# A mixture of experts in a fused kernel: GpSimd's scatter six tiles behind its gather in place of eight

## What is computed

```python
logits = t @ Wg.T + bg                              # t: 4096 tokens x 256, after a layer norm
topw, topi = jax.lax.top_k(jax.nn.softmax(logits), 2)   # 2 of 8 experts
topw = topw / jnp.sum(topw, axis=-1, keepdims=True)
...
h = t @ w1e.T                                       # 256 -> 512
gate, up = jnp.split(h, 2, axis=-1)
o = (jax.nn.silu(gate) * up) @ w2e.T                # 256 -> 256
acc = acc + ce[:, None] * o                         # ce: the token's weight for this expert
```

## Time and profile before

| | us |
|---|---|
| median of 3 runs | 1506.12 (1502.98 to 1509.09) |
| the profiled execution | 1513.09 |
| its span | 1511.3 |
| PE busy | 1179.3 (78% of the span) |
| DVE busy | 902.4 (60%) |
| ACT busy | 619.1 (41%) |
| GpSimd busy | 550.5 (36%) |

### The profile page before, as it was taken

One profiled execution on the slowest core, in us unless ns is written; L12 is line 12 of the kernel. 1 busy time (PEld: TensorE's weight loads), 2 busy tenths in 40 slices (PEclk: granted clock), 3 DMA queues, 4 the chain that ended last, 5 costly groups with the idle time before them and its releaser, 6 DMA issues. The chain is left out here.

```text
span 1511.3 us, 35117 instructions
## 1 busy us (share of the span) xinstructions
PE 1179.3 (78%) x13860; PEld 807.7 (53%) x13861; DVE 902.4 (60%) x1889; ACT 619.1 (41%) x1319; POOL 550.5 (36%) x536
## 2 busy tenths in 40 slices
PE   5999999953888888367988989797987539888860
PEld 3566666642666766134544545454545427676750
DVE  4677776757444544456668585766853474444445
ACT  2333333213344444143636446363652324444436
POOL 1333333120566665224051341405311216666640
PEclk9999999967899999588999989999997869999995
DMA  7122222039322222100000000000000482222238
GB/s 291 42 87 85 85 85 71 29 115 376 107 87 87 83 84 76 56 28 3 29 3 29 30 2 30 3 29 3 2 2 3 154 314 83 85 89 83 84 93 303
DMA packets 62424, 125.88 MB, mean 83 GB/s; under 512 B 7632, under 2 KB 43216, under 8 KB 59344
## 3 DMA queue, kind: packets, MB, share of 16 engines
q1 hardware_dynamic: 48464, 86.20, 16.2%
q0 software_dynamic: 13824, 37.77, 7.9%
HBM read 79.90 MB, written 44.04 MB: 82 GB/s over the span
## 5 line engine op out<-in xcount | busy, mean ns | idle before, releaser
L996 POOL DMA_INDIRECT ffn_xs<-xn_rows,ffn_from_row x144 | 140.0, 972 | 168.2 <-DVE ffn_to_row L1371 79.7
L1002 POOL DMA_INDIRECT y_rows<-ffn_ys,ffn_to_row x144 | 142.5, 990 | 84.7 <-DVE ffn_ys L1410 59.9
L1153 PE MATMUL ffn_ps_h<-ffn_w_high,ffn_xst 128*128 x576 | 161.3, 403 | 1.2 <-DVE ffn_xst L1404 0.6
L1394 DVE TENSOR_TENSOR ffn_act_in<-ffn_silu_g,ffn_ps_h 128x256 f32<-128x256 f32 x144 | 60.4, 420 | 160.1 <-ACT ffn_silu_g L1036 99.7
L1036 ACT ACTIVATE ffn_silu_g<-ffn_ps_h 128x256 f32<-128x256 f32 x144 | 56.4, 392 | 164.7 <-PE ffn_ps_h L1153 134.0
L1172 PE MATMUL ffn_ps_o<-ffn_w,ffn_act_t 128*128 x288 | 120.5, 441 | 0.5 <-DVE ffn_act_t L1399 0.5
L1153 PEld LDWEIGHTS ffn_ps_h<-ffn_w_high,ffn_xst 128*128 128x128 f32 x576 | 100.8, 194 | 21.5 <-issue 2.6
L1162 PE MATMUL ffn_ps_a<-ffn_constants,ffn_act_in 128*128 128x128 f32 x288 | 56.6, 278 | 55.2 <-DVE ffn_act_t L1399 55.2
L1735 POOL TENSOR_TENSOR rec_mixed_w<-rec_mixed_w,rec_xnt 128x512 f32<-128x512 f32 x16 | 17.2, 1091 | 219.3 <-DVE rec_mixed_w L2510 219.3
L2030 PE MATMUL rec_odd<-rec_mixed_w,home 128*128 128x512 f32 (+1 forms) x96 | 59.7, 760 | 45.2 <-DVE rec_mixed_r L2510 40.8
L1153 PE MATMUL ffn_ps_h<-ffn_w_low,ffn_xst 128*128 x288 | 91.2, 398 | 0.0
(11 more groups left out here) (320 smaller groups left out, 2824.2 us busy)
## 6 DMA issues: line engine op xcount, KB each, us to landing
home<-y_rows SPq DMA_DIRECT2D x20, 512.0 KB, 5.4
ffn_w_high<-w_split SPq DMA_DIRECT2D x8, 1024.0 KB, 8.4
ffn_w_low<-w_split SPq DMA_DIRECT2D x8, 1024.0 KB, 10.9
ffn_w<-w_split SPq DMA_DIRECT2D x8, 1024.0 KB, 13.9
ret_w_raw<-in_f_w SPq DMA_DIRECT2D x12, 512.0 KB, 6.4
w_split<-ret_w_high SPq DMA_DIRECT2D x12, 512.0 KB, 2.7
w_split<-ret_w_low SPq DMA_DIRECT2D x12, 512.0 KB, 4.4
xn_rows<-home SPq DMA_DIRECT2D x10, 512.0 KB, 12.3
```

The lines of the kernel that those rows point to most:

```text
L996: pool.indirect_dma_start(xs[:, n % UNROLL, :], None, xn_rows[:], bass.IndirectOffsetOnAxis(ap=from_row[:, n:n + 1], axis=0)) \
L1002: pool.indirect_dma_start(y_rows[:], bass.IndirectOffsetOnAxis(ap=to_row[:, m:m + 1], axis=0), ys[:, m % UNROLL, :], None).then_inc(ys_sto ...
L1153: mm = pe.matmul(ps_h[:, u % 2, :], one_pass(xst[:, u % 2, part, k, :]), one_pass(w1[w_part][k][:, bass.ds(e, E_COLUMNS)]), start=(part + ...
L1394: dve.tensor_tensor(act_in[:, u % 2, :], silu_g[:, u % 2, :], ps_h[:, u % 2, FF:2 * FF], ALU.mult) \
```

## The change

The distance between gather and scatter on GpSimd's queue gets a name, BEHIND = UNROLL + LAG = 6, where it was 2 * UNROLL = 8. Turn n issues gather n and then scatter n - 6. The waits of each DMA, the buffers and all other engines' programs are the same.

```diff
 UNROLL = 4
...
 LAG = 2
+BEHIND = UNROLL + LAG
...
-                for n in range(NTILES + 2 * UNROLL):
+                for n in range(NTILES + BEHIND):
                     if n < NTILES:
                         if n >= UNROLL:
                             pool.wait_ge(xst_in_psum, n - UNROLL + 1)
...
-                    m = n - 2 * UNROLL
+                    m = n - BEHIND
                     if m >= 0:
                         pool.wait_ge(ys_ready, 1 + m + 1)
```

## The result

The changed kernel takes 1531.55 us (median of 4 runs, 1531.12 to 1531.70), the kernel before 1507.61 us (4 runs, 1502.98 to 1509.24). The ratio is 1.0163 (95% interval 1.0139 to 1.0188), about 24 us more. The profiled executions are 1531.7 us (span 1529.9) against 1513.09 us (span 1511.3): 18.6 us more. All of it lies in the two expert loops: from the first scatter to the last (72 in each loop), the starts in the trace are 210.1 and 211.6 us apart before and 219.6 and 221.4 us after, 19.3 us more in sum.

What follows compares the result with a forecast made beforehand. The expert loops were taken as bound by waits, 3.08 us a tile, with GpSimd's indirect DMAs holding back PE's results. Median 1506 us, plus 27 for longer holds and 0 for gather leads, gave 1533 us; range 1476 to 1566 us.

Steps and rivals of the forecast that it cites:

- PE's results are held back beside GpSimd's DMAs: Expert loops: PE's results reach other engines up to 2.8 us late, released 2.0 to 2.1 us behind a DMA's start.
- An unbroken run: GpSimd's queue: some four indirect DMAs with only 0.30 us between them were taken to hold back PE's results.
- The hole at the gather: GpSimd's wait for PE's transpose, 1.4 us a cycle, goes; the scatter, waiting for PE's output product, is late next.
- The run ends one gather later, cycle 10.6 us: GpSimd's queue: runs stop at scatters only, making the three-tile cycle 10.6 us against 9.35 by the same sum, 1.27 longer.
- four pairs, 3.3 us a tile: Alternative in the expert loops: runs become four pairs long, 3.3 us a tile, 27 us added by another way.
- Half of the gather is lost, 27 us: Expert loops: half of the gather's 1.27 us lost, 0.64 us a cycle, 27 us in all; 1515 to 1545 us.
- 53 us: Upper end for both expert loops: a whole gather with its gap, 1.27 us, lost in each of 42 cycles.
- The lead of the gathers costs nothing: Gathers before PE's transposes: issued later, spare time falls from 7.7 to 1.0 us but holds; cost 0.
- The third rival: Expert loops: the additional gather lies inside a hold no longer for it; no change, 1506 us, chance 0.20.
- the rule beside it: Trainium skill's SBUF rule: DMA never contends with compute engines; by it the gather and scatter order costs PE nothing.
- The second rival: Expert loops: the hole at the gather was the bound; faster, 3.08 to 2.56 us a tile, 1441 us; chance 0.20.
- The signs: Expert loops: waits only at scatters, near 2.5 us or longer; SiLU 2 to 3 us late every three or four tiles.

Runs made afterwards that it cites:

- spg: Kernel before, with SP's plain loads of consecutive rows in place of GpSimd's indirect gathers; 1443.51 us, ratio 0.9543.
- spgd2: Kernel before with SP's plain loads for PE, plus GpSimd gathers into an unread buffer, on a chip with holds; 1557.18 us, ratio 1.0275.
- tinyg2: Kernel before with each gather fetching 32 of 256 columns, on a chip with holds; 1515.07 us, ratio 1.002.
- pause8: Kernel before with a GpSimd fill of a spare 128 x 1024 buffer ahead of every second gather; 1521.29 us, ratio 1.0052.
- b9: Scatter nine tiles behind the gather, against eight in the kernel before; 1505.42 us, ratio 0.9949.
- after2: The change itself (six tiles) run again on another chip, against the kernel before; 1541.47 us, ratio 1.0162.
- after3: The change itself (six tiles) run a third time, against the kernel before; 1541.22 us, ratio 1.021.
- b7: Scatter seven tiles behind the gather, against eight in the kernel before; 1539.49 us, ratio 1.0186.
- b10: Scatter ten tiles behind the gather, against eight in the kernel before, on the quick chip; 1438.06 us, ratio 0.9996.
- tinyg: Kernel before with each gather fetching 32 of 256 columns, on the quick chip; 1441.16 us, ratio 1.0019.
- spgd: Kernel before with SP's plain loads for PE, plus GpSimd gathers into an unread buffer, on the quick chip; 1457.08 us, ratio 1.0115.
- b5: Scatter five tiles behind the gather, against eight in the kernel before, on the quick chip; 1549.29 us, ratio 1.0764.

## Why the prediction was right, and which of its steps were not

1533 us was forecast and 1531.55 us came, slower by 1.6% where the sum said 1.8%. Step by step:

- **What bounds the kernel: PE's results are held back beside GpSimd's DMAs.** Right where there is a hold. spg without gathers and spgd2 with useless ones (0.954 and 1.0275) show that it is the DMAs, and tinyg2 that it isn't the gathers' bytes. "An unbroken run" is not shown: pause8 broke it with a fill and the hold came all the same. And the last stretch of the loop, where tiles pass in 2.1 us, is no support for it, since PE has only 9 instructions a tile there where it has 14 in the loop.
- **The hole at the gather goes, and the scatter is late next.** Right in both halves: 20.8 us at the gather became 2.1 us, 18.6 us at the scatter became 41.9 us, 2.8 us each. b9 is the same step the other way round.
- **The run ends one gather later, cycle 10.6 us.** Right that it ends at a gather behind a scatter, wrong in length in the profile of the change. The sum kept three pairs; the rows have four, in 12.51 us, and so do 13 of 16 stretches of the first loop and 9 of 18 of the second. The prediction named this case last: four pairs, 3.3 us a tile, 27 us in all. The measured cycle has 3.13 us a tile, since release and next scatter came 2.4 and 1.1 us apart in place of 2.1 and 2.1. Not all cycles are so long: 142 tiles cost 19.3 us more, 0.136 us each, where the forecast had 27/126 = 0.21. Nor is it so in every trace of the change: in after2 and after3 three pairs are as frequent (9 and 7, 8 and 8 stretches of some 18 in a loop) as four (6 and 8, 8 and 9), and b7 has mostly three, 10.2 and 10.3 us from pause to pause, near the 10.6 us of the sum. All are 1.6 to 2.1% slower. Common to them is not the length of the run but the pause at the scatter, 2.4 to 2.8 us in the mean in place of 1.3 and 1.4 us at the gather.
- **Half of the gather is lost, 27 us.** The term came out (18.6 us in the profiled executions, 24 between the medians), yet its mechanism, one result more getting through in a cycle of three tiles, isn't what the rows show: in the profile of the change 17 pauses a loop of 2.5 to 2.8 us took the place of 20 of 1.3 to 1.4 us. That the size is right is luck in good part: the half was a choice between nothing and 53 us, and no run measures it.
- **The lead of the gathers costs nothing.** This step failed: the cover does not hold. The text has the gathers come "one pair later, about 3 us"; its own sum moves the gather from 450.90 to 457.69 us, two pairs, and that is what came: from the issue of a gather to its transposes it was 10.0 us in the mean of a loop before, and is 3.8 and 4.3 us after (7.6 and 7.5 us in b7). The sum had 1.0 us to spare for one tile and asked that GpSimd not slide. It slides: at 430.55 us PE waits 0.60 us for a gather, 6.4 us in 8 waits in 180 us, and 25.0 us against 13.5 over the kernel. That the waits are there is measured; that they don't add to the time is what b7 speaks for, where they are absent and the ratio (1.0186) is no lower. They seem to stand in the place of waits at the activations' transposes, which fell from 24.4 to 16.6 us.
- **The third rival and the rule beside it.** SBUF — State Buffer, section Who interferes with whom, of the Trainium skill has it that "PE and ACT never wait on anyone" and that DMA never contends with a compute engine; by it spgd2 would cost no more than its own instructions. The section is about the ports of SBUF. Taken as the prediction took it, for all waiting, the runs on the chips with holds disagree: spgd2 is at 1.0275 where spg was at 0.9543, and PE's waits are 26.6 us against 0.4. Whether the hold has to do with SBUF's ports at all, no run tells. On the quick chip nothing disagrees with the sentence.
- **The second rival, 1441 us, faster.** Wrong for this change on these chips, but its number is real: 1438 to 1444 us is what the loops give wherever nothing is held (spg, and b10, tinyg and the kernel before on the quick chip).
- **The signs.** Waits at the scatter of 2.5 us and longer, SiLU 2 us late or more in 12 and 14 of 56 tiles, about one in four: seen. "Over 200 us from the first scatter to the last gather": 206.51 us.

**What stays open.** The trace doesn't assign all of the added time: from 400 to 580 us PE's waits are 26 us in sum after (16.6, 6.4, and small ones) for some 56 tiles and 24.4 us before for 59, which is 0.05 us a tile of an added 0.15 or so; where the rest lies isn't shown (the recorded ends of matmuls are modelled). What in the chip holds PE's results, what starts a hold (pause8 says that it isn't simply the lack of a 1.1 us break), and why there are none on the quick chip, no run told. The kernel before has no trace there: that nothing of it is held is concluded from its time and from the traces of the other kernels. The change wasn't seen on such a chip. Of the distances that were timed, nine is best on a chip with holds (0.995); ten was timed only on the one without, where it makes no difference.

## What to carry to other kernels

When engines wait for one another's results and none is busy all the time, look at when a result is made and when its only waiter starts, not only at the named releaser: here 1 to 3 us lay between them in the held tiles, and without the holds (spg) the kernel took 70 us less. In a queue that serves both ends of a pipeline, put distance between the two so that the wait that stops the queue is the one soonest fulfilled; pulling the second half nearer to its producer turned a short wait for the first stage (1.3 to 1.4 us) into a long one for the last (2.5 us and more). And time such an order on more than one chip.

## What the runs showed of the hardware

Not expected: the very same kernel takes 1507 to 1514 us on four occasions and 1438.68 us (19 runs) on one chip, with the granted clock the same (0.91 for the kernel before in the first profile, 0.907 to 0.916 in its runs on the quick chip). The difference, 69 to 75 us, is as large as what taking the gathers off GpSimd gains on a chip of the first kind, and there are no late SiLUs on the quick chip in tinyg, spgd or b5 and 1 and 5 of 56 tiles in b10. An indirect DMA of 128 rows takes GpSimd 0.97 to 0.99 us, with 0.30 us to the next, whether a row has 1 KB or 128 bytes; two of them, 2.56 us, are longer than PE's step of 2.51 us, so GpSimd's issuing is the next bound once nothing is held: tinyg, without holds, passes the first 64 scatters at 2.57 us a tile, and spg, without gathers on GpSimd, at 2.50.
